# Second phase of an attention and feed-forward kernel: normalising and the output's own-token part move from VectorE to ScalarE, GpSimd's additions are halved, and every engine's step order is new

## The chip, the cores and the metric

The kernel runs on one NeuronCore of a Trainium2 chip (trn2), in one launch. The metric is the device time of one execution in microseconds (us). Five engines run side by side, each through its own list of instructions in order: TensorE (PE; PEld is its weight load), VectorE (DVE), ScalarE (ACT), GpSimd (POOL) and SyncE (SP), which only issues DMAs here. They wait for one another on semaphores.

## The reference

The input is x, 8 batches of 1024 tokens with 256 features. A pre-norm attention (2 query heads, one key and value head of width 128, rotary embedding, causal mask) is added to x; then a feed-forward part on the normalised tokens is added to that. The second is what the change touches:

```python
x = x + _L0_attn_ref(_layernorm(x), ...)
x = x + _L0_ffn_ref(_layernorm(x), ...)

# _L0_ffn_ref(x, ...):
global_context = x.mean(axis=1, keepdims=True)
gf = _global_net(global_context, ...)          # 256 -> 128 -> 64 -> 1, gelu, gelu, sigmoid
out = x
for _ in range(3):
    tf = _coupling_net(out, ...)               # 256 -> 256 -> 128 -> 64 -> 1, gelu x3, sigmoid
    combined = 0.7 * gf + 0.3 * tf
    coupling = 0.1 + adaptive_range * (combined - 0.5) * 2.0
    out = out + coupling * _twist(out)
return out
```

Twisting twice gives minus the vector, so after any cycle `out` is a*x0 + b*twist(x0), where x0 is the normalised token and a and b are two numbers for each token. The output of a token is x + a*x0 + b*twist(x0).

## The kernel before

The first phase (`attention_phase`) is the attention; it ends at about 510 us and is touched only in its last steps. The second phase (`ffn_phase`) takes the 64 tiles of 128 tokens in 16 groups of four tiles (G = 4), group m holding tiles 4m to 4m+3. Two groups are one batch. Each engine walks a list of steps written out by hand, `PERIODS`, once for each n. A step is (kind, ahead, index) and works on group m = n + ahead. Four groups or more are in flight at once, and `x0`, `made`, `rstd` have SLOTS = 4 buffers. The three cycles of one group lie in successive periods. The steps, for one group:

- **stats**: VectorE takes mean and variance of the four tiles (`ffn_moments`, L216 to L222), GpSimd raises the variance to the power -0.5 (`ffn_rstd`, L229).
- **scale**: VectorE writes x0 = (x - mean) * rstd, four instructions of 128x256 (`ffn_scale`, L237). It waits until the slot's former group, m-4, has its output, since that reads the old x0. TensorE's turn waits for all four.
- **turn**: TensorE transposes x0 (L1275), ScalarE copies it out of PSUM as the high half with a row sum (L1076), VectorE subtracts to get the low half (L1157).
- **product** 0 to 3: TensorE multiplies with w1 and its sign-twisted form, six matmuls each (L1291 to L1293); ScalarE copies each result to `made` (L1084).
- **global** 0 to 2: in each second group alone, a chain of three tiny products, each followed by a ScalarE function (L1305, L1310, L1314; L1091, L1094, L1099); VectorE then makes `base_coupling` (L1163).
- **spread** 1, 2: TensorE spreads a and b over the partitions (L1334). It waits for VectorE's `squash` of the cycle before.
- **mix** 1, 2: VectorE multiplies the spread numbers with `made` (L1172, L1175), GpSimd adds the parts over 128x1024 (L1053).
- **gelu1**, **h2**, **h3**: ScalarE's gelu of two halves (L1111), a product (L1345) with a gelu (L1118), a product (L1353, L1357) with a gelu (L1125).
- **dot** and **squash**: GpSimd multiplies with w4 (L1060), VectorE sums (L1183), ScalarE takes a tanh (L1134), VectorE updates a and b in a few instructions of 128x4 (`update_state`, L1225 to L1259).
- **final** 0 to 3, one for each tile: VectorE makes y_part = a*x0 + x (L1196), then adds b*twist(x0) in two instructions of 128x128 (L1204, L1207). After all four, SP stores the group (L1027).

What matters of the order before: VectorE's list is scale(0), stats(1), turn(0), dots, squashes, mix(-1,1), mix(-2,2), final(-3, 0 to 3). TensorE's is turn(0), h3(-2,1), global 0, h3(-3,2), global 1, and in the next period product 0 of the same group, global 2, product 1, both spreads, product 2, h2 of cycle 0, product 3, h3 of cycle 0, h2 of cycles 1 and 2, and the next turn.

## Time and profile before

| | us |
|---|---|
| median of 3 runs (893.6 to 894.84) | 894.32 |
| the profiled execution's own time | 893.9 |
| its span, first to last instruction | 892.4 |
| first phase, to the first instructions of the second | 510.3 |
| turn of the first group to turn of the last (15 periods) | 313.7 |
| from the last turn to the end | 68.4 |

1.5 us of the execution lie outside its span. A row of the trace has a start and a duration in us from the span's start, the engine, the line, the operation, what it writes and reads, and in brackets the idle time ahead of it with what ended that. "PEclk" is the TensorE clock that was granted, as a share of 2.4 GHz: 0.50 is the level of 1.2 GHz. A period here is the time from the start of one turn (L1275) to the next. One where the group of the starting turn closes a batch also has the global steps; it is called a global period below.

### The profile page before, as it was taken

To read this page: it belongs to the slowest core of one execution; us is meant where nothing else is said; L and a number is where in the kernel's file an instruction comes from. 1 tells how busy PE (TensorE), PEld (TensorE's weight loads), DVE (VectorE), ACT (ScalarE), POOL (GpSimd) and SP (SyncE) were. 2 spreads that over 40 slices of the span, in tenths; PEclk is the share of its full clock that TensorE was granted. 3 is DMA by queue.
4 is the path that set the end of the run, shared out by engine and by line. 5 is a ranking of instruction groups with operands and counts; after the bars stand their busy time and mean duration, and the time that the engine had idled before them with its cause. 6 is when DMAs were issued, how large, how long until landed. Compare 5 with 4: busy or idle time off the path is not lost. (4 is left out here: it accounts for less than half of the span.)

```text
span 892.4 us, 13579 instructions
## 1 busy us (share of the span) xinstructions
PE 782.7 (88%) x4240; PEld 638.8 (72%) x4240; DVE 720.0 (81%) x1695; ACT 463.6 (52%) x1020; POOL 365.0 (41%) x375
## 2 busy tenths in 40 slices
PE   4679999999999999999999789888888979898952
PEld 3568888888887888888888666666666757675731
DVE  5879898998998989979988737786977696868675
ACT  2445665556565665565656346554544454445431
POOL 3536634564266345642560014343433333333331
PEclk9899999999999999999999989988988797979775
DMA  6000011001100110011000080000100010101011
GB/s 193 1 1 19 30 49 48 18 31 48 48 25 25 48 48 24 25 48 48 1 1 1 18 265 1 21 27 15 35 24 14 11 48 1 44 5 48 1 48 48
DMA packets 34570, 32.43 MB, mean 36 GB/s; under 512 B 3524, under 2 KB 34244, under 8 KB 34500
## 3 DMA queue, kind: packets, MB, share of 16 engines
q1 hardware_dynamic: 34500, 31.56, 11.1%
q8 instruction: 36, 0.59, 0.3%
q14 instruction: 34, 0.28, 0.1%
HBM read 16.88 MB, written 14.68 MB: 35 GB/s over the span
## 5 line engine op out<-in xcount | busy, mean ns | idle before, releaser
L507 ACT ACTIVATE pT_hi<-bank 128x512 fp32r<-128x512 f32 x192 | 91.2, 492 | 98.7 <-PE bank L846 90.5
L554 ACT ACTIVATE x_all<-scores_ps,neg_max 128x384 f32<-128x384 f32 (+7 forms) x128 | 94.7, 740 | 37.5 <-DVE neg_max L690 37.1
L581 DVE TENSOR_TENSOR pT_lo<-bank,pT_hi 128x512 fp32r<-128x512 f32 x192 | 100.7, 548 | 13.5 <-ACT pT_hi L507 12.4
L846 PE MATMUL bank<-ident,x_all 128*128 128x128 f32 x576 | 91.6, 276 | 20.3 <-DVE pT_lo L581 19.8
L690 DVE CUSTOM_DVE_ANT_0 scores_ps<-scores_ps,x 128x384 f32<-128x384 f32 (+7 forms) x128 | 96.6, 760 | 14.6 <-PE scores_ps L740 14.0
L1345 PE MATMUL cycle_ps<-h,w_sb 128*128 128x512 f32 x192 | 93.5, 624 | 12.5 <-ACT h L1111 12.5
L384 POOL TENSOR_TENSOR rope_a<-x_all,cos_sb 128x384 f32<-128x384 f32 x60 | 61.7, 1028 | 103.2 <-ACT x_all L507 98.9
L846 PEld LDWEIGHTS bank<-ident,x_all 128*128 128x128 f32 x576 | 67.7, 140 | 35.6 <-DVE pT_lo L581 26.3
L1060 POOL TENSOR_TENSOR h_w<-h,w_sb 128x256 f32<-128x256 f32 x48 | 36.5, 762 | 102.6 <-ACT h L1125 102.6
L738 PE MATMUL oT_ps<-pT_hi,v_hi 128*128 128x512 f32 x192 | 75.9, 395 | 1.3 <-issue 1.0
L1345 PEld LDWEIGHTS cycle_ps<-h,w_sb 128*128 128x128 f32 x192 | 36.4, 198 | 47.7 <-issue 25.2
L1053 POOL TENSOR_TENSOR mixed<-part_b,made 128x1024 f32<-128x1024 f32 x16 | 38.1, 2378 | 79.3 <-DVE part_b L1175 79.3
L738 PE MATMUL scores_ps<-k_hi,q_hi 128*128 128x512 f32 (+1 forms) x192 | 69.9, 364 | 0.4 <-ACT x_all L554 0.2
L1291 PE MATMUL made_ps<-x0T_hi,w_hi 128*128 128x512 f32 x128 | 67.2, 525 | 2.8 <-DVE x0T_lo L1157 2.6
L483 POOL TENSOR_TENSOR rope_b<-x_all,sin_sb 128x384 f32<-128x384 f32 x64 | 66.6, 1040 | 1.3 <-ACT x_all L507 0.8
L497 POOL TENSOR_TENSOR rot<-rope_a,rope_b 128x384 f32<-128x384 f32 x64 | 66.2, 1035 | 1.9 <-DVE rope_a L384 1.8
L740 PE MATMUL oT_ps<-pT_hi,v_lo 128*128 128x512 f32 x192 | 66.8, 348 | 0.0
L740 PE MATMUL scores_ps<-k_hi,q_lo 128*128 128x512 f32 (+1 forms) x192 | 66.7, 347 | 0.0
L739 PE MATMUL oT_ps<-pT_lo,v_hi 128*128 128x512 f32 x192 | 66.7, 347 | 0.0
L739 PE MATMUL scores_ps<-k_lo,q_hi 128*128 128x512 f32 (+1 forms) x192 | 66.5, 346 | 0.0
L465 POOL TENSOR_TENSOR rstd<-var_eps,minus_half 128x4 f32<-128x4 f32 x16 | 16.3, 1017 | 117.5 <-DVE var_eps L639 117.5
L1118 ACT ACTIVATE h<-cycle_ps,b_sb 128x512 f32<-128x512 f32 x48 | 33.1, 690 | 59.5 <-PE cycle_ps L1345 59.5
(129 smaller groups left out, 2165.2 us busy)
## 6 DMA issues: line engine op xcount, KB each, us to landing
x_all<-x SPq DMA_DIRECT2D x16, 512.0 KB, 4.0
out<-x_all SPq DMA_DIRECT2D x16, 512.0 KB, 2.9
x<-x_all SPq DMA_DIRECT2D x12, 512.0 KB, 2.9
x_all<-x SPq DMA_DIRECT2D x6, 1024.0 KB, 7.2
x_all<-wqkv SPq DMA_DIRECT2D x1, 512.0 KB, 5.2
sin_sb<-sin_t SPq DMA_DIRECT2D x1, 512.0 KB, 7.0
cos_sb<-cos_t SPq DMA_DIRECT2D x1, 256.0 KB, 5.8
x_all<-wo SPq DMA_DIRECT2D x1, 256.0 KB, 5.4
```

Source lines behind the costliest of these rows:

```text
L483: pool.tensor_tensor(rope_b[:].rearrange("p (c e d) -> p c e d", e=2, d=HALF), qk[:, :, ::-1, :], sin.rearrange("p c (e d) -> p c e d", e= ...
L497: pool.tensor_tensor(rot[:, t, :], rope_a[:], rope_b[:], ALU.add).then_inc(rot_ready, 1)
L507: return nc.scalar.activation(out, in_, ACT.Copy)
L554: nc.scalar.activation(probs[u % 2][:, k, 0:keys], scores_ps[k % 2][:, 0:keys], ACT.Exp, bias=neg_max[:, u * G + k:u * G + k + 1], scale=-1.0,
L581: return dve.tensor_tensor(out, whole, hi.bitcast(F32), ALU.subtract)
L690: dve.tensor_tensor_reduce(out=masked, in0=masked, in1=mask_row[:, T - keys:], scale=-1.0, scalar=LARGEST, op0=ALU.add, op1=ALU.min, accum ...
L738: nc.tensor.matmul(out, stationary[0], moving[0], start=first, stop=False)
L739: nc.tensor.matmul(out, stationary[0], moving[1], start=False, stop=False)
L740: return nc.tensor.matmul(out, stationary[1], moving[0], start=False, stop=last)
L846: mm = nc.tensor.transpose(ps[:, k * P:(k + 1) * P], probs[u % 2][:, k, j * P:(j + 1) * P], ident[:])
L1291: nc.tensor.matmul(ps[:], hi, x0T_hi[:, k, :], start=k == 0, stop=False)
L1345: mm = nc.tensor.matmul(cycle_ps[c][:], f.w2_sb[:, k, :], h1[c][:, k, :], start=k == 0, stop=k == DC - 1)
```

## The change

- `ffn_scale` moves to ScalarE: x0 = rstd*x + shift, as an Identity activation with a scale and a bias for each partition. VectorE makes shift = -mean*rstd first, one instruction of 128x4 for each group (`ffn_shift`). For group 0 both sit at the end of the first phase; ScalarE's four activations stand ahead of its seventh copy of the last unit of scores.
- VectorE's y_part goes. ScalarE writes (1 + a*rstd)*x + a*shift over x, four activations for each group (step **blend**), and VectorE's final adds the twist in place. VectorE makes the scale and the bias in three more instructions of 128x4 at the end of the third squash.
- GpSimd's mix is two additions of 128x512, each with its own semaphore count, and ScalarE's gelu of a half waits for that half.
- All lists have a new order. TensorE's and GpSimd's steps are also counted one or two groups later, which alone moves nothing, since their lists are cyclic. From the turn on, TensorE's is: turn(0), h3(-2,1), h3(-3,2), global 0, 1, 2, product 0, spread of cycle 1, product 1, spread of cycle 2, products 2 and 3, h2 of cycles 0 and 1, h3 of cycle 0, h2 of cycle 2, next turn.

```diff
@@ ffn_scale
-def ffn_scale(dve, f, m, slot, x0, x_tiles):
+def ffn_shift(dve, f, m, slot):
 
     dve.wait_ge(f.rstd_ready, m + 1)
+    dve.scalar_tensor_tensor(out=f.shift[slot][:], in0=f.moments[slot][:, :, 0], scalar=-1.0,
+                             in1=f.rstd[slot][:], op0=ALU.mult,
+                             op1=ALU.mult).then_inc(f.shift_ready, 1)
+
+
+def ffn_scale(act, f, m, slot, x0, x_tiles):
+
+    act.wait_ge(f.shift_ready, m + 1)
     for t in range(G):
-        dve.tensor_scalar(x0[:, t, :], x_tiles[t], f.moments[slot][:, t, 0:1],
-                          f.rstd[slot][:, t:t + 1], ALU.subtract, ALU.mult).then_inc(f.x0_ready, 1)
+        act.activation(x0[:, t, :], x_tiles[t], ACT.Identity, bias=f.shift[slot][:, t:t + 1],
+                       scale=f.rstd[slot][:, t:t + 1]).then_inc(f.x0_ready, 1)
@@ PERIODS
     "tensor": [
-        ("product", -1, 0), ("global", -1, 2), ("product", -1, 1), ("spread", -2, 1),
-        ("spread", -3, 2), ("product", -1, 2), ("h2", -1, 0), ("product", -1, 3), ("h3", -1, 0),
-        ("h2", -2, 1), ("h2", -3, 2), ("turn", 0, 0), ("turn", 0, 1), ("h3", -2, 1),
-        ("global", 0, 0), ("h3", -3, 2), ("global", 0, 1),
+        ("product", -2, 3), ("h2", -2, 0), ("h2", -3, 1), ("h3", -2, 0), ("h2", -4, 2),
+        ("turn", -1, 0), ("turn", -1, 1), ("h3", -3, 1), ("h3", -4, 2), ("global", -1, 0),
+        ("global", -1, 1), ("global", -1, 2), ("product", -1, 0), ("spread", -2, 1),
+        ("product", -1, 1), ("spread", -3, 2), ("product", -1, 2),
     ],
     "scalar": [
-        ("product", -1, 3), ("h3", -1, 0), ("h2", -2, 1), ("h2", -3, 2), ("turn", 0, 0),
-        ("turn", 0, 1), ("global", 0, 0), ("h3", -2, 1), ("h3", -3, 2), ("global", 0, 1),
-        ("squash", -2, 1), ("squash", -1, 0), ("global", 0, 2), ("squash", -3, 2),
-        ("product", 0, 0), ("product", 0, 1), ("gelu1", 0, 0), ("h2", 0, 0), ("gelu1", -1, 1),
-        ("product", 0, 2), ("gelu1", -2, 2),
+        ("gelu1", -3, 2), ("scale", 0), ("h2", -2, 1), ("h3", -1, 0), ("h2", -3, 2), ("turn", 0, 0),
+        ("turn", 0, 1), ("h3", -2, 1), ("product", -1, 3), ("h3", -3, 2), ("global", 0, 0),
+        ("squash", -1, 0), ("global", 0, 1), ("global", 0, 2), ("squash", -2, 1), ("squash", -3, 2),
+        ("product", 0, 0), ("blend", -3), ("product", 0, 1), ("gelu1", 0, 0), ("gelu1", -1, 1),
+        ("product", 0, 2), ("h2", 0, 0),
     ],
     "vector": [
-        ("scale", 0), ("stats", 1), ("turn", 0, 0), ("turn", 0, 1), ("dot", -2, 1), ("dot", -1, 0),
-        ("dot", -3, 2), ("squash", -2, 1), ("global", 0, 2), ("squash", -1, 0), ("squash", -3, 2),
-        ("mix", -1, 1), ("mix", -2, 2), ("final", -3, 0), ("final", -3, 1), ("final", -3, 2),
-        ("final", -3, 3),
+        ("final", -4, 1), ("shift", 0), ("final", -4, 2), ("final", -4, 3), ("stats", 1),
+        ("turn", 0, 0), ("turn", 0, 1), ("dot", -1, 0), ("dot", -2, 1), ("global", 0, 2),
+        ("squash", -1, 0), ("dot", -3, 2), ("squash", -2, 1), ("squash", -3, 2), ("mix", -1, 1),
+        ("mix", -2, 2), ("final", -3, 0),
     ],
     "gpsimd": [
-        ("dot", -1, 0), ("stats", 1), ("dot", -2, 1), ("dot", -3, 2), ("mix", -1, 1),
-        ("mix", -2, 2),
+        ("mix", -3, 1), ("mix", -4, 2), ("dot", -2, 0), ("dot", -3, 1), ("dot", -4, 2),
+        ("stats", 0),
     ],
@@ gpsimd, mix
-                        pool.tensor_tensor(mixed_sb[c][:], part_b[c][:], other,
-                                           ALU.add).then_inc(mix_ready[c], 1)
+                        for k in range(DC):
+                            pool.tensor_tensor(mixed_sb[c][:, k, :], part_b[c][:, k, :],
+                                               other[:, k, :], ALU.add).then_inc(mix_ready[c], 1)
@@ scalar
+                    if kind == "scale":
+
+                        at_least(act, x0_turned, (m - SLOTS + 1) * DC)
+                        at_least(act, y_ready, (m - SLOTS + 1) * (2 * G))
+                        ffn_scale(act, f, m, slot, x0[slot], [x_tile(m, t) for t in range(G)])
+                    if kind == "blend":
+
+                        act.wait_ge(blend_ready, m * 2 + 2)
+                        for t in range(G):
+                            x = x_tile(m, t)
+                            act.activation(x, x, ACT.Identity, bias=blend_shift[:, t:t + 1],
+                                           scale=blend_scale[:, t:t + 1]).then_inc(blended, 1)
@@ scalar, gelu1
                         for k in range(DC):
+                            if c > 0:
+                                act.wait_ge(mix_ready[c], m * DC + k + 1)
@@ vector, final
-                        at_least(dve, y_ready, (m * G + t) * 2)
-                        dve.scalar_tensor_tensor(out=y_part[:], in0=x0[slot][:, t, :],
-                                                 scalar=a_b[:, 0, t:t + 1], in1=x_tile(m, t),
-                                                 op0=ALU.mult, op1=ALU.add).then_inc(y_part_ready, 1)
-                        dve.wait_ge(y_part_ready, m * G + t + 1)
+                        dve.wait_ge(blended, m * G + t + 1)
@@ vector, update_state of the third cycle
+                at_least(dve, blended, m * G)
+                dve.tensor_tensor(x_scale[:], new[:, 0, :], f.rstd[slot][:],
+                                  ALU.mult).then_inc(x_scale_ready, 1)
+                dve.tensor_tensor(blend_shift[:], new[:, 0, :], f.shift[slot][:],
+                                  ALU.mult).then_inc(blend_ready, 1)
                 dve.tensor_scalar(minus_b[:], new[:, 1, :], -1.0, None,
                                   ALU.mult).then_inc(minus_b_ready, 1)
+                dve.wait_ge(x_scale_ready, m + 1)
+                dve.tensor_scalar(blend_scale[:], x_scale[:], 1.0, None,
+                                  ALU.add).then_inc(blend_ready, 1)
```

## Rows read from the trace of the kernel before

**Rows 1.** The page: busy time, share of the span, instructions; the clock in tenths.

```profile
span 892.4 us, 13579 instructions
PE 782.7 (88%) x4240; PEld 638.8 (72%) x4240; DVE 720.0 (81%) x1695; ACT 463.6 (52%) x1020; POOL 365.0 (41%) x375
...
PEclk9899999999999999999999989988988797979775
```

**Rows 2.** Windows, one per period: length, busy us of each engine, PEclk, DMA.

```profile
557.26:579.27 22.01, 19.58 (x96) 14.20 (x94) 16.11 (x36) 11.99 (x27) 7.87 (x6) 0.92 0.03 9
579.27:599.42 20.15, 17.78 (x84) 13.32 (x84) 17.62 (x44) 11.10 (x23) 8.27 (x6) 0.92 0.08 27
599.42:624.38 24.96, 22.63 (x95) 17.35 (x96) 18.01 (x45) 11.35 (x26) 8.22 (x6) 0.79 0.07 22
...
668.13:691.32 23.19, 20.86 (x83) 15.97 (x83) 17.70 (x44) 10.97 (x23) 8.22 (x6) 0.78 0.07 23
...
716.24:735.10 18.86, 16.43 (x84) 11.91 (x84) 17.51 (x44) 10.98 (x23) 8.16 (x6) 1.00 0.09 29
...
sum 266.74, PE 238.32 PEld 179.06 DVE 210.91 ACT 134.75 POOL 98.24; mean PE 19.86 PEld 14.92 DVE 17.58 ACT 11.23 POOL 8.19
```

**Rows 3.** Timeline of the period from 716.24 us.

```profile
716.24 1.10 PE L1275 MATMUL made_ps<-ident,x 128*128 128x128 f32 x8 [2.33 <-DVE x L237]
716.94 0.60 ACT L1076 ACTIVATE x0T_hi<-made_ps 128x512 fp32r<-128x512 f32 x1 [2.30 <-PE made_ps L1275]
...
719.35 0.38 ACT L1125 ACTIVATE h<-cycle_ps 128x256 f32<-128x256 f32 x1 [0.63 <-PE cycle_ps L1357]
...
722.70 0.17 DVE L1259 TENSOR_SCALAR minus_b<-state 128x4 f32<-128x4 f32 x1
...
722.96 1.23 DVE L1175 TENSOR_TENSOR part_b<-cycle_ps,made 128x1024 f32<-128x1024 f32 x1
723.15 1.34 ACT L1111 ACTIVATE h<-made,b_sb 128x512 f32<-128x512 f32 x2
...
726.36 0.56 DVE L1196 SCALAR_TENSOR_TENSOR y_part<-x,state,x_all 128x256 f32<-128x256 f32 x1
726.59 2.58 POOL L1053 TENSOR_TENSOR mixed<-part_b,part_a 128x1024 f32<-128x1024 f32 x1
...
726.95 2.36 DVE L1204 SCALAR_TENSOR_TENSOR x_all<-x,state,y_part 128x128 f32<-128x128 f32 x1
...
730.14 0.35 DVE L1204 SCALAR_TENSOR_TENSOR x_all<-x,state,y_part 128x128 f32<-128x128 f32 x1
730.40 0.35 DVE L1207 SCALAR_TENSOR_TENSOR x_all<-x,minus_b,y_part 128x128 f32<-128x128 f32 x1
...
733.66 1.38 DVE L237 TENSOR_SCALAR x<-x_all,f_moments,f_rstd 128x256 f32<-128x256 f32 x4
...
735.10 1.09 PE L1275 MATMUL made_ps<-ident,x 128*128 128x128 f32 x8 [2.34 <-DVE x L237]
```

**Rows 4.** Windows around the clock's changes, columns as in Rows 2.

```profile
557.26:562.10 4.84, 4.74 (x39) 4.48 (x38) 1.58 (x3) 2.90 (x9) 1.50 (x3) 1.00 0.00 2
562.10:565.50 3.40, 3.40 (x10) 2.35 (x9) 1.96 (x10) 1.41 (x5) 0.61 (x1) 0.50 0.00 0
...
667.92:678.16 10.24, 10.03 (x37) 9.06 (x38) 6.12 (x25) 3.40 (x10) 2.47 (x3) 0.50 0.12 41
```

**Rows 5.** ScalarE by line, 557 to 824 us: count, busy us, mean ns, idle ahead.

```profile
L1111 ACT ACTIVATE h<-mixed,b_sb 128x512 f32<-128x512 f32 x48 | 31.8, 713 | 0.0
L1084 ACT ACTIVATE made<-made_ps 128x512 f32<-128x512 f32 x48 | 28.2, 587 | 10.2 <-PE made_ps L1293 10.2
L1118 ACT ACTIVATE h<-cycle_ps,b_sb 128x512 f32<-128x512 f32 x37 | 25.5, 690 | 41.3 <-PE cycle_ps L1345 41.3
...
L1125 ACT ACTIVATE h<-cycle_ps 128x256 f32<-128x256 f32 x36 | 13.7, 381 | 16.2 <-PE cycle_ps L1357 15.8
```

**Rows 6.** Window from the last turn to the end, columns as in Rows 2.

```profile
824.00:892.38 68.38, 40.93 (x172) 28.65 (x172) 43.68 (x102) 21.00 (x46) 18.17 (x13) 0.71 0.11 36
```

More of the change, by code:

```diff
@@ L204, in __init__ @@
         self.rstd = [sb(f"f_rstd{n}", [P, G]) for n in range(SLOTS)]
+        self.shift = [sb(f"f_shift{n}", [P, G]) for n in range(SLOTS)]
         self.first_x0 = sb("x0_0", [P, G, D])
@@ L563, in do @@
                         r = (FIRST_STEP[u] + j) % PT_RING
+                        if isinstance(b, int) and b == B and j == G + 2:
+                            act.wait_ge(max_ready, B * BATCH_SCORES)
+                            ffn_scale(act, f, 0, 0, f.first_x0,
+                                      [f.x_all[:, t, :] for t in range(G)])
                         act.wait_ge(p_turned, m + 1)
@@ L910, in period_steps @@
             continue
-        if kind in ("stats", "scale") and isinstance(n, int) and n + ahead == 0:
+        if kind in ("stats", "shift", "scale") and isinstance(n, int) and n + ahead == 0:
             continue
@@ L978, in ffn_phase @@
         base_coupling = [sb(f"base_coupling{n}", [P, 1]) for n in range(2)]
-        y_part = sb("y_part", [P, D])
+        x_scale = sb("x_scale", [P, G])
+        blend_scale = sb("blend_scale", [P, G])
+        blend_shift = sb("blend_shift", [P, G])
         made_ps = [psum(f"made_ps{n}", [P, G * P]) for n in range(3)]
@@ L1009, in ffn_phase, with x_tile @@
         minus_b_ready = sem("minus_b_ready")
-        y_part_ready = sem("y_part_ready")
+        x_scale_ready = sem("x_scale_ready")
+        blend_ready = sem("blend_ready")
+        blended = sem("blended")
         y_ready = sem("y_ready")
         y_stored = sem("y_stored")
+        def x_tile(m, t):
+            return x_all[:, m * G + t, :]
         block = ctx.enter_context(nc.Block())
@@ L1148, in do @@
                         ffn_moments(dve, f, m, slot, [x_tile(m, t) for t in range(G)])
-                    if kind == "scale":
-                        at_least(dve, x0_turned, (m - SLOTS + 1) * DC)
-                        at_least(dve, y_ready, (m - SLOTS + 1) * (2 * G))
-                        ffn_scale(dve, f, m, slot, x0[slot], [x_tile(m, t) for t in range(G)])
+                    if kind == "shift":
+                        at_least(dve, f.x0_ready, (m - SLOTS + 1) * G)
+                        ffn_shift(dve, f, m, slot)
                     if kind == "turn":
```

19 lines of the change are left out of this document (7 added, 12 removed).

## The prediction, made before the changed kernel was run

> **What bounds the kernel now.** I read the page first. The span is 892.4 us, and in its last 18 slices, the second phase, TensorE's clock falls to 7 to 9 tenths, while it is full through most of the first [rows 1]. So the second phase has something that the first has not. I then cut it at the turns. From 557.26 to 824.00 us twelve periods take 266.74 us, 22.2 us each, and they are of very different length [rows 2]. The six that are not global take 18.8 us three times, 20.2 us twice and 23.2 us once, 20.0 us in the mean; of the six global ones five take 24.9 to 25.0 us and one takes 22.0 us, 24.45 us in the mean. The clock column sorts them: 1.00, 0.92, 0.78 to 0.80. No engine is full. TensorE is busy 16.43 us of an 18.86 us period at full clock, VectorE 17.5 us, ScalarE 11.2 us, GpSimd 8.2 us.
>
> The timeline says what closes the circle [rows 3]. TensorE does its turn at 716.24 and must stand idle for 2.34 us ahead of the next at 735.10, until VectorE has written x0. VectorE's part: its squashes end at 722.87 (the last small one starts at 722.70 and takes 0.17), the mixes run 722.96 to 726.4, the finals 726.36 to 733.6, the scale 733.66 to 735.04. So the loop is: turn to mix 6.72 us, mixes 3.4, finals 7.2, scale and handing over 1.5: 18.86. The finals take so long because of one instruction: L1204 takes 2.36 us at 726.95 and 0.35 at 730.14. It stands while GpSimd's addition of 2.58 us, from 726.59, runs. Thus VectorE and GpSimd shut each other out.
>
> The same idle time has a second price. The clock is at its lower level (0.50, that is 1.2 GHz) from 667.92 to 678.16, right behind a period's idle time, and once at 562.10 for 3.4 us without idle time: the stretch before is 4.74 us busy of 4.84, but with the turn, the narrow h3 matmuls and the global steps [rows 4]. Half clock costs 4.3 us in a period for 10.24 us of it (23.19 against 18.86), 1.3 for 3.4 us (20.15 against 18.86) [rows 2]: 0.4 us for each us of it.
>
> **The change, part by part, over one period at full clock.**
>
> *Scale.* VectorE loses 1.38 us. But x0 has four buffers, and scale(m) still waits for all four finals of m-4: the link stays in the loop. ScalarE's price isn't in the trace. Nearest rows: 381 ns for 128x256 without a pointer operand; a bias pointer adds 690 - 587 = 103 ns at 128x512; the whole 128x512 from SBUF is 713 [rows 5]. So 381 + 2 x 103 = 587 ns, less some 90 of overlap (two L1111 of 0.713 take 1.34 us together [rows 3, 5]), is 0.50 us each. Bounds are 0.38 and 0.71. Four are 2.1 us (1.5 to 2.9), in place of 1.38.
>
> The Trainium skill (ScalarE: Activation LUTs, Rules for kernel authors) says to do add and multiply on VectorE, not on ScalarE. By that rule this move loses time, and the rows agree that an instruction gets dearer. What counts here is in whose list it stands; and ScalarE has 11 us of work in 22.
>
> *y_part and blend.* VectorE loses 4 x 0.48 to 0.56, 2.1 us with the handing over, out of the loop [rows 3]. ScalarE gains 4 x 0.50 = 2.0 us ahead of product 1's copy. ScalarE's load becomes 11.2 + 4.1 = 15.3 us. blend waits for the third squash, so product 1's copy and the gelu of cycle 0 come some 3 us later than their data, and TensorE, which wants that gelu after four products, waits about 0.8 us there; that is inside the slack TensorE has. The four added small ones on VectorE at 0.17 us each, three in the chain of the third squash, add 0.4 us to it, and shift adds 0.2 to the finals.
>
> *Halves of mix.* Two of about 1.25 us instead of one of 2.4 to 2.6. Fixed cost of the second: 0.1 to 0.2 us, hidden. The gelu of the first half may start 1.2 us earlier; that isn't on the loop, the finals are. The shut-out of VectorE stays, since finals and addition meet as before, and they exclude each other for the same total of 2.5 us. Bounds: nothing gained, or 1.2 us gained if a half falls elsewhere. I take nothing.
>
> The Trainium skill (SBUF — State Buffer, Who interferes with whom) states that a VectorE instruction with two SBUF inputs and a GpSimd one that reads SBUF exclude each other for the whole instruction. L1204's 2.36 us agrees. By that rule the new finals are still open to it.
>
> *Order.* ScalarE now does three evacuations (h2, h3, h2: 0.65 + 0.35 + 0.65) between scale and turn, and product 3's between two h3. Before, its turn copy began 0.70 us behind the turn; now it begins 1.65 us behind the scale, and the h3 of cycle 2 is done 0.65 us later than at +3.49 [rows 3]. For that TensorE waits 0.6 us ahead of product 0.
>
> The loop now: turn to mix 6.72 + 0.65 + 0.4 = 7.8; mixes 3.5; finals 7.15 - 2.1 - 0.25 (a small shut-out with dot, which has moved away) + 0.2 = 5.0; scale 2.1 and handing over 0.1. That is **18.5 us** against 18.86. The bounds of ScalarE's price make it 17.9 to 19.2. TensorE needs 16.5, so it waits 2.0 us a period still, but in three pieces under 0.9 us, and only 0.4 ahead of the turn.
>
> *Global periods.* TensorE's global 0, 1, 2 now stand in a row, with nothing between them to cover the trips to ScalarE and back, and ScalarE's copy of product 3, a h3 and a tanh stand in between. I count base_coupling, and with it the mix, 1.4 us later: 19.9 us at full clock. The six global periods before are 20.6 by the same reckoning (22.0 - 1.4).
>
> *The clock.* With only 0.4 us idle ahead of the turn I expect no fall in the other periods: 18.5. In the global ones turn, narrow matmuls and waits are some 6 us of light work, and the fall at 562.10 came so: I expect it in each, four times for 3.4 us (21.3) and twice for 10.24 (24.2). Twelve periods: 6 x 18.5 + 4 x 21.3 + 2 x 24.2 = 244.6, that is **-22 us**.
>
> *Ends.* At the end of the first phase four activations on ScalarE hold back two copies of scores, which VectorE's 1.38 us didn't: +0.5. Between 510 and 557 the first scale waits behind an h2: +0.6 by estimate, against as much gained by four products in a row: 0 in all. SP's list is the old one, and no DMA is moved. Behind the last turn, 68.4 us [rows 6]: one global period, -1.5 as above; three joins of mix and gelu in the drain, 0.6 each (second half 1.25 + one gelu 0.7 in place of two gelus); last finals without y_part, -1.4, small ones +0.4. Say -4.
>
> Sum: 893.9 - 22 - 4 = 868 for the profiled kind of execution; the median lies 0.4 above the profiled one's own time. I forecast **868 us**.
>
> **Rivals.**
> 1. *The clock stays full.* If global periods don't fall either: 6 x 18.5 + 6 x 19.9 = 230.4, -36, ends -5: **853**. For it: idle pieces under 1 us. Against: 562.10.
> 2. *The clock falls as often as now.* 6 others: 18.5 + (2 x 1.4 + 4.3)/6 = 19.7; global: 19.9 + (5 x 4.3 + 1.4)/6 = 23.7; sum 260, -6.5, ends -3: **884**. For it: a turn, two h3 and two waits are still light work.
> 3. *Slower: TensorE's idle time only moves behind the turn and keeps the clock low.* The wait for product 0, with h3 and turn ahead of it, makes each period long: 22.8 and 24.2 give 282, +15, ends -2: **907**. It decides from a mean period of 22.5 us. For it: ScalarE's list now stands between turn and product 0. Against: idle time falls from 2.34 to 2.0 us and is split.
> 4. *Nothing.* A dearer scale (0.71 each, +0.75 us a period) with rival 2 takes the gain: about 893.
>
> **Numbers.** Forecast 0.45, its own range 857 to 877; rival 1 0.18; rival 2 0.20; rival 3 0.13; rival 4 0.04. A measurement of this kernel tells 0.2% (1.8 us) from no change. Faster 0.83, same 0.04, slower 0.13. For 8 in 10 I go from 846 (rival 1 with the cheap activation) to 888.
>
> **What would show it.** Right: L237 gone, TensorE's idle time ahead of L1275 under 1 us and ended by ScalarE; periods without global steps near 18.5 at PEclk 1.00; new activations of about 0.5 to 0.6 us; a final's instruction still stretched to about 1.3 us beside a half addition; ScalarE busy about 15 us a period. Wrong: half clock in the periods without global steps; finals ending with GpSimd out of the way (then under 17.9); new waits on ScalarE for blend or scale that end with VectorE and are longer than 1 us; another table load.

## The result: 841.8 us against 894.6, and the profile after

The changed kernel takes 841.83 us (median of 4 runs, 840.5 to 842.96), the kernel before 894.58 us beside it (893.6 to 895.0). The ratio is 0.9411, with an interval from 0.9391 to 0.9431. The forecast was 868 us with a range from 846 to 888, so the time fell by twice what was forecast, 53 us instead of 26, and came out 4 us below the range. The forecast had the sign and the mechanism, but it had the length of the loop wrong, and what the clock does in the global periods.

The page of the changed kernel, to be read beside [rows 1]: busy times, and the clock by slice.

```profile
span 839.0 us, 13716 instructions
PE 752.3 (90%) x4240; PEld 612.5 (73%) x4240; DVE 658.6 (78%) x1631; ACT 525.6 (63%) x1148; POOL 365.7 (44%) x407
...
PEclk9899999999999999999999998999999999999975
```

Between the first phase and the drain the clock row now hardly leaves 9. TensorE does the same 4240 matmuls in 752 us instead of 783, because fewer of them run at half clock. VectorE has lost 61 us and ScalarE has gained 62.

The windows by period of the changed kernel (columns as in [rows 2]); of twelve, six are shown, and the first, third and fifth of these are global.

```profile
558.59:578.45 19.86, 19.16 (x96) 14.39 (x94) 14.08 (x40) 15.10 (x35) 8.33 (x8) 0.91 0.07 23
578.45:595.31 16.86, 16.46 (x85) 11.91 (x84) 14.03 (x39) 14.81 (x32) 8.32 (x8) 1.00 0.11 37
...
667.21:687.08 19.87, 19.17 (x96) 14.38 (x94) 13.99 (x40) 15.19 (x35) 8.29 (x8) 0.91 0.07 23
687.08:703.94 16.86, 16.45 (x84) 11.92 (x84) 14.02 (x39) 14.88 (x32) 8.34 (x8) 1.00 0.11 37
703.94:722.38 18.44, 17.74 (x96) 13.23 (x95) 13.99 (x40) 15.26 (x35) 8.35 (x8) 1.00 0.08 28
722.38:739.12 16.74, 16.42 (x84) 11.86 (x83) 14.04 (x39) 14.69 (x32) 8.32 (x8) 1.00 0.10 34
...
sum 217.50, PE 210.85 PEld 155.36 DVE 166.59 ACT 179.89 POOL 99.85; mean PE 17.57 PEld 12.95 DVE 13.88 ACT 14.99 POOL 8.32
```

Twelve periods take 217.50 us instead of 266.74. The six without global steps take 16.7 to 17.1 us, all at PEclk 1.00. Of the six global ones two take 18.44 us at full clock and four 19.87 at 0.91. In a period of 16.86 us TensorE is busy 16.45: the engine that waited for VectorE before is now the bound itself.

The timeline of the period from 687.08 us shows the circle of [rows 3] again, and that it no longer closes on TensorE.

```profile
686.93 0.67 ACT L1154 ACTIVATE h<-cycle_ps,b_sb 128x512 f32<-128x512 f32 x1
...
687.08 1.09 PE L1308 MATMUL made_ps<-ident,x 128*128 128x128 f32 x8
687.50 0.36 ACT L1161 ACTIVATE h<-cycle_ps 128x256 f32<-128x256 f32 x1
687.77 0.67 ACT L1154 ACTIVATE h<-cycle_ps,b_sb 128x512 f32<-128x512 f32 x1
...
688.34 0.58 ACT L1112 ACTIVATE x0T_hi<-made_ps 128x512 fp32r<-128x512 f32 x1
...
689.15 1.00 PE L1390 MATMUL cycle_ps<-w_sb,h 128*128 128x64 f32 x8
...
690.22 0.41 ACT L1161 ACTIVATE h<-cycle_ps 128x256 f32<-128x256 f32 x1
...
690.49 0.47 PE L1324 MATMUL made_ps<-x0T_hi,w_hi 128*128 128x512 f32 x1 [0.35 <-ACT made L1120]
...
693.08 0.16 DVE L1281 TENSOR_TENSOR state<-state,scaled 128x4 f32<-128x4 f32 x1
...
693.56 1.22 DVE L1210 TENSOR_TENSOR part_b<-cycle_ps,made 128x1024 f32<-128x1024 f32 x1
...
693.69 2.08 ACT L1105 ACTIVATE x_all<-x_all,blend_shift,blend_scale 128x256 f32<-128x256 f32 x4 [0.80 <-DVE blend_scale L1292]
...
697.13 0.43 DVE L1234 SCALAR_TENSOR_TENSOR x_all<-x,state,x_all 128x128 f32<-128x128 f32 x1
...
697.37 2.60 POOL L1077 TENSOR_TENSOR mixed<-part_b,part_a 128x512 f32<-128x512 f32 x2
697.49 1.36 DVE L1237 SCALAR_TENSOR_TENSOR x_all<-x,minus_b,x_all 128x128 f32<-128x128 f32 x1
...
698.77 1.35 DVE L1234 SCALAR_TENSOR_TENSOR x_all<-x,state,x_all 128x128 f32<-128x128 f32 x1
...
700.38 0.34 DVE L1234 SCALAR_TENSOR_TENSOR x_all<-x,state,x_all 128x128 f32<-128x128 f32 x1
...
700.91 0.34 DVE L1234 SCALAR_TENSOR_TENSOR x_all<-x,state,x_all 128x128 f32<-128x128 f32 x1
701.17 0.34 DVE L1237 SCALAR_TENSOR_TENSOR x_all<-x,minus_b,x_all 128x128 f32<-128x128 f32 x1
...
701.59 2.07 ACT L247 ACTIVATE x<-x_all,f_shift,f_rstd 128x256 f32<-128x256 f32 x4
702.17 1.94 PE L1378 MATMUL cycle_ps<-h,w_sb 128*128 128x512 f32 x4
...
703.94 0.82 PE L1308 MATMUL made_ps<-ident,x 128*128 128x128 f32 x6
```

The turn at 703.94 has no bracket: its matmuls wait for nothing. Its x0 was ready at 703.66, 0.28 us earlier, and TensorE was still at L1378. (Only the weight load ahead of it, which has no row here, was held for x0, until 703.72.) The one wait of TensorE left in the period is 0.35 us at 690.49, for ScalarE. Read as in the prediction, the loop is: turn to mix 6.48 us, mixes 3.57, finals 4.38 (697.13 to 701.51), scale and handing over 2.15. That is 16.6 us, just under the 16.8 us of TensorE's own circle, its 16.45 us of work and the wait of 0.35.

### The profile page after: what moved, and what is told of

It reads as the page before. It is cut to its first block and busy times, and to the rows that moved or that the text cites. A ratio compares the mean times of both kernels' runs of the same rounds, so it can differ in the third digit from the quotient of the medians.

```text
span 839.0 us, 13716 instructions
## 1 busy us (share of the span) xinstructions
PE 752.3 (90%) x4240; PEld 612.5 (73%) x4240; DVE 658.6 (78%) x1631; ACT 525.6 (63%) x1148; POOL 365.7 (44%) x407
## 5 line engine op out<-in xcount | busy, mean ns | idle before, releaser
L1378 PE MATMUL cycle_ps<-h,w_sb 128*128 128x512 f32 x192 | 94.2, 628 | 11.3 <-ACT h L1147 11.1
L1378 PEld LDWEIGHTS cycle_ps<-h,w_sb 128*128 128x128 f32 x192 | 35.9, 198 | 49.4 <-issue 30.2
L1324 PE MATMUL made_ps<-x0T_hi,w_hi 128*128 128x512 f32 x128 | 57.9, 452 | 4.6 <-ACT made L1120 3.0
L1192 DVE TENSOR_TENSOR x0T_lo<-made_ps,x0T_hi 128x512 fp32r<-128x512 f32 x32 | 20.6, 686 | 52.4 <-ACT x0T_hi L1112 52.4
L517 ACT ACTIVATE x_all<-bank 128x512 f32<-128x512 f32 x64 | 38.1, 596 | 34.1 <-PE bank L754 34.1
```

The lines of the kernel that those rows point to most:

```text
L517: return nc.scalar.activation(out, in_, ACT.Copy)
L1378: mm = nc.tensor.matmul(cycle_ps[c][:], f.w2_sb[:, k, :], h1[c][:, k, :], start=k == 0, stop=k == DC - 1)
```

## The experiments

Sixteen runs were made, one of them the changed kernel once more, each with the kernel before on the same chip. The chips differ by up to 0.5%, so times of different groups are best compared by their ratios. The kernel before took 889.83 us beside the order alone, the old order, the filled kernel and the whole additions, 893.52 beside the rest of part 2, 892.62 beside two and six extra instructions, TensorE's old list and the drain, 893.39 beside the last four. "Period" means one without global steps, where nothing else is said.

**1. Where the 53 us come from.** First the parts: all operations as before in the new order, all new operations in the old order, and the kernel before with nothing but extra matmuls on the idle TensorE.

*Order alone* (scale back on VectorE, y_part back, whole additions):

```diff
@@ scalar, against the changed kernel's list
-        ("gelu1", -3, 2), ("scale", 0), ("h2", -2, 1), ("h3", -1, 0), ("h2", -3, 2), ("turn", 0, 0),
+        ("gelu1", -3, 2), ("h2", -2, 1), ("h3", -1, 0), ("h2", -3, 2), ("turn", 0, 0),
...
-        ("product", 0, 0), ("blend", -3), ("product", 0, 1), ("gelu1", 0, 0), ("gelu1", -1, 1),
+        ("product", 0, 0), ("product", 0, 1), ("gelu1", 0, 0), ("gelu1", -1, 1),
@@ vector
-        ("final", -4, 1), ("shift", 0), ("final", -4, 2), ("final", -4, 3), ("stats", 1),
+        ("final", -4, 1), ("final", -4, 2), ("final", -4, 3), ("scale", 0), ("stats", 1),
```

> The instructions of before (scale and y_part on VectorE, whole additions), in the new order; VectorE's scale stands behind the last final. Theory A (the period is the longer of TensorE's work, 16.5 us, and the loop turn - squashes - mix - finals - scale - turn; the clock falls only behind idle time of TensorE or in global steps): loop 6.3 + 3.65 + 4.4 + 2.1 for y_part + 1.5 for scale = 17.95, so 1.1 us idle ahead of the turn, a clock that falls in global periods alone: 850 to 860 us. Rival B (the order does nothing, the moved instructions do it all): 888 to 895. Rival C (the order does it all): 842 to 845.

It took 886.38 us against 889.83 before, ratio 0.994 (0.9901 to 0.9978). That is outside all three ranges, between theory A and rival B. A period at full clock:

```profile
668.78:687.20 18.42, 16.41 (x84) 11.87 (x84) 17.54 (x44) 11.19 (x23) 8.12 (x6) 1.00 0.09 30
```

Theory A had 17.95 us for it with 1.1 us idle ahead of the turn. It is 18.42 with 1.91 idle, and the clock falls in four of the six periods, where A had it fall in global ones alone.

*New operations in the old order* (scale ahead of the turn and blend ahead of product 1 in ScalarE's list, shift in scale's old place on VectorE; GpSimd's power stands behind the dots, since its wait for the blend's scale asks for that; all else in the lists as before):

```diff
@@ scalar
-        ("gelu1", -3, 2), ("scale", 0), ("h2", -2, 1), ("h3", -1, 0), ("h2", -3, 2), ("turn", 0, 0),
+        ("product", -1, 3), ("h3", -1, 0), ("h2", -2, 1), ("h2", -3, 2), ("scale", 0),
...
-        ("product", 0, 0), ("blend", -3), ("product", 0, 1), ("gelu1", 0, 0), ("gelu1", -1, 1),
+        ("product", 0, 0), ("blend", -3), ("product", 0, 1), ("gelu1", 0, 0), ("h2", 0, 0), ("gelu1", -1, 1),
```

> The instructions of after (scale and blend on ScalarE, halves) in the order of before; blend stands behind product 0, scale right ahead of ScalarE's turn copy, GpSimd's power behind the dots, which blend forces. Theory A: loop 6.7 + 0.4 (small instructions) + 3.6 + 4.6 + 2.2 = 17.5, idle 1 us ahead of the turn: 848 to 858 us. Rival B (the moved instructions do it all): 842 to 845. Rival C (the order does it all): 885 to 895.

It took 933.85 us, ratio 1.0496 (1.0445 to 1.0546): slower than either kernel, and far outside all three ranges. Its timeline, at a full-clock period of 21.3 us:

```profile
754.90 2.08 ACT L1105 ACTIVATE x_all<-x_all,blend_shift,blend_scale 128x256 f32<-128x256 f32 x4 [1.02 <-DVE blend_scale L1292]
...
758.88 1.98 PE L1378 MATMUL cycle_ps<-h,w_sb 128*128 128x512 f32 x4 [2.12 <-ACT h L1147]
...
762.27 0.34 DVE L1237 SCALAR_TENSOR_TENSOR x_all<-x,minus_b,x_all 128x128 f32<-128x128 f32 x1
...
767.33 2.06 ACT L247 ACTIVATE x<-x_all,f_shift,f_rstd 128x256 f32<-128x256 f32 x4
...
769.44 0.33 PE L1308 MATMUL made_ps<-ident,x 128*128 128x128 f32 x1 [2.74 <-ACT x L247]
```

The blend stands ahead of cycle 0's gelu, and TensorE waits 2.12 us for that. VectorE's finals end at 762.6, but scale starts at 767.33, since it is queued behind gelus whose matmuls come late. So neither half of the change, as run here, is worth much alone (-3 us and +44 us); together they give -53. The +44 holds for this one way of putting the new steps into the old lists: the blend alone in the old order, with scale left on VectorE, was not run, so how much a better place for them would save there is open.

*The kernel before with its idle time filled*: ten matmuls of 128x384 whose result nobody reads, ahead of the turn's wait.

```diff
+                        if c == 0 and isinstance(n, int) and 4 <= n < NGROUPS:
+                            for _ in range(10):
+                                nc.tensor.matmul(global_ps[:, P:4 * P], f.w1_hi[0][:, 0, 0:P],
+                                                 f.w1_hi[0][:].rearrange("p c n -> p (c n)")[:, 0:3 * P],
+                                                 start=True, stop=True)
                         pe.wait_ge(f.x0_ready, m * G + G)
```

> The kernel before, with ten matmuls of 128x384 on weights, their product used by nobody, ahead of TensorE's wait for x0 in each turn from group 4 on: about 1.7 us at full clock inside 2.3 us of idle time. Nothing else is changed. Theory A (the idle time has a second price, the clock): the clock stays full in periods without global steps, 18.9 us each, global ones 20.6 to 22: 862 to 875 us, faster with more work. Rival (the clock falls for another reason, the light matmuls of turn and h3): as before or slower, 894 to 910.

It took 863.36 us against 889.83, ratio 0.9703 (0.9655 to 0.975), as theory A has it. Two of its windows, columns as in [rows 2]:

```profile
658.35:677.18 18.83, 18.14 (x93) 13.67 (x93) 17.50 (x44) 10.98 (x23) 8.17 (x6) 1.00 0.09 29
677.18:697.62 20.44, 19.84 (x106) 15.04 (x106) 17.93 (x45) 11.42 (x26) 8.23 (x6) 1.00 0.08 27
```

The loop is as long as before (18.83 us), but every period without global steps is now at full clock, with TensorE idle 0.60 us ahead of the turn instead of 2.34. So about 26 of the 53 us are the price of the clock alone. The rest is the loop: from 18.86 to 16.85 us and from 20.4 to 18.4 us is 2.0 us in each of twelve periods, 24 us, less 1.4 for one short fall of the clock more in the changed kernel's global periods (four against three); the ends give what is left.

**2. Which of the operations matters.** From the changed kernel one was undone at a time.

*Scale back on VectorE* (behind the last final; all else as changed):

```diff
@@ vector
-        ("final", -4, 1), ("shift", 0), ("final", -4, 2), ("final", -4, 3), ("stats", 1),
+        ("final", -4, 1), ("shift", 0), ("final", -4, 2), ("final", -4, 3), ("scale", 0), ("stats", 1),
```

> The changed kernel with scale on VectorE again (four instructions behind the last final); blend, halves and order stay. Theory A (period = the longer of TensorE's work and the loop): in the changed kernel VectorE's finals end 14.4 us behind the turn, and TensorE wants x0 at 16.8; 1.4 us of scale on VectorE fit, and ScalarE's copies come earlier: 836 to 842 us, idle ahead of the turn under 0.3 us. Rival (taking scale off VectorE was needed): 850 or more.

839.85 us (839.65 to 840.3), as theory A has it, where the changed kernel, run beside it, took 842.75 (841.98 to 844.12). *The changed kernel again:*

> The changed kernel once more, as the yardstick for the three beside it on one chip: 840 to 844 us.

The ratios to before are 0.9402 (0.9367 to 0.9437) and 0.9437 (0.9406 to 0.9468). Moving scale was not needed; the version without that move is the fastest measured, by 0.3%, though the intervals of the ratios overlap. Its period:

```profile
686.83:703.56 16.73, 16.40 (x84) 11.85 (x83) 16.30 (x47) 12.81 (x27) 8.35 (x8) 1.00 0.11 37
```

The Trainium skill (ScalarE: Activation LUTs, Rules for kernel authors) gives adds and multiplies to VectorE. The rows agree for this step: four such instructions take 2.07 us on ScalarE (L247) and took 1.38 us on VectorE [rows 3]. The next experiment shows where the rule didn't decide.

*y_part back on VectorE* (no blend, scale stays on ScalarE):

```diff
-                        dve.wait_ge(blended, m * G + t + 1)
+                        dve.scalar_tensor_tensor(out=y_part[:], in0=x0[slot][:, t, :],
+                                                 scalar=a_b[:, 0, t:t + 1], in1=x_tile(m, t),
+                                                 op0=ALU.mult, op1=ALU.add).then_inc(y_part_ready, 1)
+                        dve.wait_ge(y_part_ready, m * G + t + 1)
...
```

> The changed kernel with y_part on VectorE again (no blend); scale on ScalarE, halves and order stay. Theory A: the finals get 2.1 us longer, the loop 16.6 + 2.1 - 0.3 = 18.4 us; TensorE idle 1.6 us ahead of the turn, clock falls in global periods and some others: 862 to 880. Rival (ScalarE, relieved of 2 us, gives it back): 842 to 850.

898.62 us, ratio 1.0067 (1.0034 to 1.0101), outside the expected range. TensorE is idle 2.1 us ahead of each turn again, and no period is at full clock (20.3 to 21.5 us, PEclk 0.84 to 0.92). The blend is what takes the loop below TensorE's work: added last, it is worth 56 us (898.62 to 842.75), more than the whole change. The two kernels with scale on VectorE say the same: 0.994 of the time before with y_part on VectorE (order alone, with whole additions), 0.940 with the blend.

*Whole additions on GpSimd* (one of 128x1024 instead of two halves):

```diff
-                        for k in range(DC):
-                            pool.tensor_tensor(mixed_sb[c][:, k, :], part_b[c][:, k, :],
-                                               other[:, k, :], ALU.add).then_inc(mix_ready[c], 1)
+                        pool.tensor_tensor(mixed_sb[c][:], part_b[c][:], other[:],
+                                           ALU.add).then_inc(mix_ready[c], DC)
```

> The changed kernel with each addition of GpSimd whole again, 128x1024. Theory A: the gelus of mixed halves have slack, and finals and addition exclude each other for the same total: 842, within 2 us. Rival (the halves let gelu and finals in earlier, and that counts): 846 or more.

844.22 us, ratio 0.9492 (0.9437 to 0.9546); its periods without global steps are 16.8 to 17.1 us, the same, and they could hardly show more, since TensorE bounds them. The time lies just outside theory A's 842 within 2. Behind the last turn it takes 64.7 us instead of 62.95, but so do others with the halves (64.8 in the next experiment). The intervals of the ratios overlap (0.9406 to 0.9468 for the changed kernel again), so these runs don't tell the halves' worth from nothing. In its periods one final alone is stretched beside GpSimd's addition:

```profile
697.85 2.47 DVE L1236 SCALAR_TENSOR_TENSOR x_all<-x,minus_b,x_all 128x128 f32<-128x128 f32 x1
```

*Global steps apart* (global 0 between the two h3, 1 and 2 behind the second, on both engines):

```diff
@@ tensor; ScalarE's list alike
-        ("turn", -1, 0), ("turn", -1, 1), ("h3", -3, 1), ("h3", -4, 2), ("global", -1, 0),
+        ("turn", -1, 0), ("turn", -1, 1), ("h3", -3, 1), ("global", -1, 0), ("h3", -4, 2),
```

> The changed kernel with global 0 between the two h3 and global 1 behind them, in TensorE's and ScalarE's lists. Theory A: TensorE loses two waits of 0.35 us in global periods and the light stretch gets shorter, so the clock falls less often (four of six before): 835 to 841. Rival (the wait is only moved to product 0, and the clock falls on the light matmuls whatever their order): 841 to 844.

845.29 us, ratio 0.946 (0.9418 to 0.9501), above both ranges: global periods of 18.7 us at full clock instead of 18.44, and the clock falls in four of six as it did. Putting them in a row costs nothing.

**3. The length of the loop.** Extra VectorE instructions of 128x256, output unused, ahead of the last final make the changed kernel's loop longer and leave all else alone.

```diff
...
+                        if t == 3:
+                            at_least(dve, spare_ready, m * 6)
+                            for s in range(6):
+                                dve.tensor_scalar(spare[:, s, :], f.w1_hi[0][:, 0, :].bitcast(F32), 1.0,
+                                                  None, ALU.mult).then_inc(spare_ready, 1)
```

Two, and then six:

> The changed kernel with 2 extra VectorE instructions (128x256, about 0.33 us each) ahead of the last final of each group; their output is not used. They lengthen the loop turn, mix, finals, scale by 0.66 us, to about 17.2 us at full clock. Theory A (a period is the longer of TensorE's own work, 16.8 us, and the loop; the clock stays full while little idle time stands ahead of the turn): about 0.4 us a period more, 16 periods, 846 to 851 us, periods without global steps 17.2 to 17.3 us at full clock. Rival (loop and TensorE's work are not separate bounds, every us added counts from the first): 842 + 16 x 0.66 = 853 us. Rival C (any idle time brings clock falls): above 860 us.

> The same with 6 extra instructions, 2.0 us, which makes the loop about 18.6 us, the length that the prediction forecast for it. Theory A: TensorE stands idle 1.7 to 2.0 us ahead of each turn; by the order-only run that is enough to bring clock falls in most periods, so periods of 18.6 us at full clock and 20 to 23 us with falls, 870 to 900 us in all. Rival (the clock would have stayed full at the forecast's length in the periods without global steps, as the prediction's sum has it): 18.5 to 18.6 in all six of those, 862 to 870 us.

They took 848.29 us (ratio 0.9498, 0.947 to 0.9527) and 857.24 us (0.960, 0.9575 to 0.9625). The first is as theory A has it; the second missed both ranges, because the extra instructions are cheaper than assumed. The row of six, and the windows of a period with two and with six:

```profile
673.64 1.29 DVE L1231 TENSOR_SCALAR spare<-w_hi 128x256 f32<-128x256 f32 x6
```

```profile
693.32:710.36 17.04, 16.63 (x84) 11.78 (x84) 14.41 (x41) 14.67 (x32) 8.33 (x8) 1.00 0.10 32
```

```profile
659.83:677.66 17.83, 16.63 (x83) 11.77 (x83) 15.20 (x45) 14.61 (x32) 8.31 (x8) 1.00 0.09 31
```

One costs 1.29 / 6 = 0.215 us. 17.04 - 2 x 0.215 = 16.61 and 17.83 - 6 x 0.215 = 16.54: the loop of the changed kernel is 16.6 us, by the timeline and by these two.

Now the lengths that the prediction had given the loop, and that of the kernel before:

> The changed kernel with 9 extra VectorE instructions (128x256, output unused) ahead of the last final. In the runs with 2 and 6 of them each took 0.215 us of the loop, and the period at full clock was 17.04 and 17.84 us, so that the loop without any is 16.6 us. With 9 it is 16.6 + 1.9 = 18.5 us, the length that the prediction gave it, and TensorE stands idle 1.7 us ahead of the turn. Theory A (the prediction's sum at its own loop length): no clock fall in the periods without global steps, 18.5 us each, global ones with short falls, 866 to 876 us in all. Theory B (1.7 us idle is enough to bring falls, as the 1.9 us of the order-only run were): falls in most periods, 20 to 23 us each, 885 to 905 us.

> The same with 12 extra instructions: loop 16.6 + 2.6 = 19.2 us, idle 2.3 us ahead of the turn, as the kernel before has it. Theory B: falls in most periods, often long ones, a mean period of 22 to 23.5 us, 900 to 920 us. Rival (the kernel before loses its clock through something else than this idle time): periods of 19.2 and 21 us with short falls alone, 875 to 885 us.

Nine made it 866.34 us (0.9717, 0.966 to 0.9774) and twelve 895.43 (1.002, 0.9997 to 1.0042). Windows of nine, and of twelve:

```profile
661.62:680.08 18.46, 16.62 (x83) 11.78 (x83) 15.71 (x48) 14.61 (x32) 8.34 (x8) 1.00 0.09 30
```

```profile
583.58:604.22 20.64, 18.26 (x84) 13.41 (x84) 16.77 (x51) 14.73 (x32) 8.32 (x8) 0.92 0.08 27
671.12:692.76 21.64, 19.36 (x83) 14.54 (x84) 16.67 (x51) 14.68 (x32) 8.33 (x8) 0.84 0.08 26
```

| extra instructions | idle ahead of the turn, us | period, us | periods with half clock, of the 6 | time, us |
|---|---|---|---|---|
| 0 | 0 | 16.85 | 0 | 841.8 |
| 2 | 0.25 | 17.04 | 0 | 848.3 |
| 6 | 1.05 | 17.83 | 0 | 857.2 |
| 9 | 1.66 | 18.46 | 1 | 866.3 |
| 12 | 2.27 | 19.1 to 21.6 | 4 | 895.4 |

With a loop of 18.46 us the kernel takes 866 us, about what the prediction forecast for 18.5, and inside the range of theory A. Its four executions lie between 863 and 873 us, the profiled one at 869. Twelve came out between its two theories, with falls in most periods but few long ones. From nine to twelve the loop grows by 0.65 us, 8 us over twelve periods, and the time by 29: there the idle time begins to cost the clock as well. The order-only kernel of part 1 has the same full-clock period as nine, 18.42 us, with the idle time in one piece of 1.91 us, where nine has 1.66 and 0.36; its clock falls in four of six periods and it takes 886 us. Whether the 0.25 us or the one piece makes that difference was not separated.

**4. Which list the new operations need.** One engine's list at a time was put back to the old order in the changed kernel: TensorE's, ScalarE's (as in the old-order kernel of part 1), VectorE's.

```diff
@@ tensor
-        ("product", -2, 3), ("h2", -2, 0), ("h2", -3, 1), ("h3", -2, 0), ("h2", -4, 2),
...
+        ("spread", -3, 2), ("product", -1, 2), ("h2", -1, 0), ("product", -1, 3), ("h3", -1, 0),
+        ("h2", -2, 1), ("h2", -3, 2), ("turn", 0, 0), ("turn", 0, 1), ("h3", -2, 1),
...
@@ vector, in the third kernel
...
-        ("turn", 0, 0), ("turn", 0, 1), ("dot", -1, 0), ("dot", -2, 1), ("global", 0, 2),
-        ("squash", -1, 0), ("dot", -3, 2), ("squash", -2, 1), ("squash", -3, 2), ("mix", -1, 1),
...
+        ("shift", 0), ("stats", 1), ("turn", 0, 0), ("turn", 0, 1), ("dot", -2, 1), ("dot", -1, 0),
+        ("dot", -3, 2), ("squash", -2, 1), ("global", 0, 2), ("squash", -1, 0), ("squash", -3, 2),
...
```

> The changed kernel with TensorE's list alone in the order of before (spreads and h2 between the products, global steps apart), the lists of ScalarE and VectorE as changed. Theory A (the gain of the order lies in the three lists fitting together): TensorE's first h2 stands behind three products and waits for a gelu that ScalarE now makes later, so idle time comes back: 845 to 870 us. Rival (the gain lies in the lists of ScalarE and VectorE alone): 842 us as the changed kernel.

> The changed kernel with ScalarE's list alone in the order of before, scale ahead of the turn and blend ahead of product 1 as in the kernel with all lists old. Theory A (ScalarE's list is where the old order fails the changed operations: the blend ahead of the gelu of cycle 0, and scale behind product 3 and three evacuations): 880 to 930 us, TensorE idle over 1.5 us ahead of its turn, ended by ScalarE's scale. Rival (TensorE's list is what costs in the old order): under 860 us.

> The changed kernel with VectorE's list alone in the order of before (first squash behind the second, dots ahead of each other as before, all four finals of a group in a row ahead of shift and stats). Theory A (VectorE's list costs little, since both orders put the same operations between turn and mix): mix starts 0.2 to 0.4 us later behind the turn and the loop is 16.8 to 17.1 us: 842 to 850 us. Rival (the squash of cycle 0 behind the second dot holds the spread and so the mix back by over 1 us): 860 us or more.

They took 879.92 us (0.9855, 0.9824 to 0.9885), 953.5 (1.0681, 1.0638 to 1.0724) and 855.78 (0.9582, 0.9547 to 0.9617). In the first two theory A has the place right, but both cost more than its ranges; the third is between its two theories. The waits of TensorE that the three bring back, one row of each timeline:

```profile
676.99 1.98 PE L1378 MATMUL cycle_ps<-h,w_sb 128*128 128x512 f32 x4 [1.69 <-ACT h L1147]
```

```profile
705.06 1.09 PE L1308 MATMUL made_ps<-ident,x 128*128 128x128 f32 x8 [2.74 <-ACT x L247]
```

```profile
663.86 0.65 PE L1367 MATMUL cycle_ps<-ident,state 128*128 128x128 f32 x4 [0.92 <-DVE state L1250]
```

With TensorE's old list the first h2 stands behind three products instead of four, and waits 1.69 us for a gelu that the blend has delayed. With ScalarE's old list scale is queued behind everything, as in part 1, and TensorE also waits 2.0 us for a gelu ahead of an h2. With VectorE's old list the squash of cycle 0 comes behind the second. The mix starts 0.42 us later behind the turn (6.90 against 6.48), about as theory A has it, but that isn't what makes the period 17.7 us: the spread waits 0.92 us for that squash, the rival's mechanism. ScalarE's list is the one that costs most, 112 us.

**5. The drain.** Behind the last turn the changed kernel still takes 62.95 us, much of it at half clock. From there on eight unused matmuls were put ahead of each spread and h2, in the kernel with scale on VectorE, where that stretch takes 62.92 us at 0.74 without them.

```diff
+                        if n >= NGROUPS + 1:
+                            for _ in range(8):
+                                nc.tensor.matmul(global_ps[:, P:4 * P], f.w1_hi[0][:, 0, 0:P],
+                                                 f.w1_hi[0][:].rearrange("p c n -> p (c n)")[:, 0:3 * P],
+                                                 start=True, stop=True)
                         pe.wait_ge(h1_ready[c], m * DC + DC)
...
```

> The changed kernel with scale on VectorE and, from the drain on only, 8 extra matmuls (128x384, result unused) ahead of each spread and each h2 wait, so that TensorE isn't idle there. Theory A (the drain, 62.9 us behind the last turn with some 30 us of it at half clock, is partly bound by the clock): 4 to 8 us less than the 840 us of that kernel, 832 to 836 us, and the periods before the drain unchanged. Rival (the drain is bound by the chain of gelus, mix and finals and not by TensorE's clock): 839 to 843 us.

844.0 us (840.2 to 846.1), ratio 0.9447 (0.9413 to 0.9481), against 839.85 and 0.9402 (0.9367 to 0.9437) without them, on another chip. Theory A's gain of 4 to 8 us didn't come, and the median is 1 us above the rival's range. The window behind the last turn, of the changed kernel and of this one:

```profile
776.09:839.04 62.95, 37.25 (x173) 25.29 (x171) 35.74 (x98) 31.32 (x66) 19.28 (x19) 0.74 0.10 34
```

```profile
776.10:842.14 66.04, 47.10 (x245) 36.66 (x243) 35.78 (x98) 30.99 (x64) 18.61 (x18) 0.88 0.10 33
```

The clock is higher, 0.88 against 0.74, and the drain isn't shorter but 3 us longer. Of these 3 us, 2 may have nothing to do with them: with the same lists and no extra matmuls it takes 62.9 us in some profiles and 64.8 to 65.0 in others (global steps apart; two and six extra instructions). That it is bound by a chain over VectorE, GpSimd and ScalarE, in which TensorE's clock matters little, fits this and was not tested further.

## Why the prediction missed, step by step

- **The loop before, and its second price: right.** The idle time ahead of the turn cost the clock; filling it alone gave 26 us.
- **Turn to mix, 7.8 us: wrong, and the largest error in the loop.** It measured 6.48, 1.3 less. The prediction added 0.65 us for ScalarE's evacuations and 0.4 for the new small instructions to the old 6.72. The turn's copy did begin late, 1.26 us behind the turn instead of 0.70. Behind the scale it is 1.41 us (686.93 to 688.34), where 1.65 was forecast: the three evacuations in a row start 0.57, 0.27 and 0.57 us apart, less than their own durations. But the last h3 was done at +3.55 us, hardly later than the old +3.49. The reason stood in [rows 3]: ScalarE had waited 0.63 us for TensorE ahead of that very h3, and a wait absorbs what comes ahead of it. The matmuls that it waits for end at +3.07 in both kernels (689.15 and 718.31, each with 1.00). The small instructions cost next to nothing: from the start of the squash's last instruction to the mix it is 0.48 us (693.08 to 693.56) where it was 0.45 (722.51 to 722.96). And from the end of the last h3 to that instruction it is 2.45 us instead of 2.78; the squash of cycle 0 now stands ahead of the last dot, and with VectorE's old list (part 4) it is 2.87. The two rows of the kernel before:

```profile
718.31 1.00 PE L1357 MATMUL cycle_ps<-w_sb,h 128*128 128x64 f32 x8
...
722.51 0.16 DVE L1256 TENSOR_TENSOR state<-state,scaled 128x4 f32<-128x4 f32 x1
```

- **Finals, 5.0 us: 0.6 too long.** They measured 4.38. From one tile's final to the next it is 0.53 us (700.38 to 700.91) where it was 1.17 (730.14 to 731.31), so a tile's y_part took 0.64 us of the list, and all four 2.5 us and not 2.1. The new shift takes 0.07 us of the list and not 0.2, and a stretched final, 0.47 us over its plain 0.35, had been taken at 0.25; against these goes 0.1 us that the two stretches beside the halves cost more than the one before. These are rows of the kernel before:

```profile
731.31 0.35 DVE L1204 SCALAR_TENSOR_TENSOR x_all<-x,state,y_part 128x128 f32<-128x128 f32 x1
731.58 0.82 DVE L1207 SCALAR_TENSOR_TENSOR x_all<-x,minus_b,y_part 128x128 f32<-128x128 f32 x1
```

- **Scale 2.1, mixes 3.5: right** (2.07 for four, 590 ns each by themselves; 3.57). That scale was worth moving was wrong, as part 2 shows. The loop of 18.5 us was thus 16.6.
- **TensorE's work: in the prediction, but not as a bound.** It had "TensorE needs 16.5" and never asked what happens if the loop comes out shorter. The period is 16.85, TensorE's 16.45 busy, a wait of 0.35 for ScalarE and little else. This is also why a further gain on VectorE or ScalarE, as in the version of 839.85 us, gives next to nothing.
- **Halves and shut-out: right.** Nothing in the periods. L1237 and L1234 take 1.36 and 1.35 us beside the two halves, where L1204 took 2.36 beside one whole [rows 3]: 2.0 us over the plain 0.35 in both; with whole additions in the changed kernel one final takes 2.47, 2.1 us over it (part 2). The Trainium skill (SBUF — State Buffer, Who interferes with whom) says that such a pair excludes each other for a whole instruction; the rows agree, and splitting one side of it only splits the wait.
- **Global periods, 19.9 us at full clock: 18.44.** That is the same error of the loop.
- **The clock: half right.** No fall in the periods without global steps, as forecast. In the global ones four short falls, as forecast, but none of the two long ones. With the loop's error this is the whole miss over twelve periods: six others 9.9 us (18.5 against 16.85), four global ones 5.7 (21.3 against 19.87), two global ones 11.5 (24.2 against 18.44), 27.1 in all. Some 18.6 of these are the loop's and 8.6 the two long falls, 4.3 each, that never came. And the reason given for the full clock, 0.4 us idle ahead of the turn and 2.0 us a period in three pieces, was not what happened: nothing is idle ahead of the turn, and 0.35 us in the period.
- **Ends, -4 us: right in sum** (510.33 to 509.50, 46.93 to 49.09, 68.38 to 62.95: -4.1), and by luck: the first phase was forecast 0.5 longer and is 0.8 shorter, the three periods before the twelve were to stay and are 2.2 longer in all, the drain was forecast about 4.3 shorter and is 5.4.
- **The rivals.** The first (the clock stays full) came nearest with 853 us. The third (slower, through idle time behind the turn) did not come: behind the turn the changed kernel waits only 0.35 us. Two of the kernels with old lists are slower than before, but through idle time ahead of the turn or ahead of an h2.

With nine extra instructions the changed kernel has the prediction's loop, and takes 866 us. So from the loop's length on, the sum stood nearly; the step from the lists to that length failed. In part that too is luck: its twelve periods take 240.6 us where the sum had 244.6, with one fall in a plain period that the sum didn't have and without the two long ones that it had, and its 1.66 us of idle time ahead of the turn are not the prediction's 0.4.

## What to carry to other kernels

When a change puts work ahead of an instruction that waits, subtract the wait that the trace shows in brackets before adding the work; and when a loop through other engines gets shorter, compare it with the busy time of the engine it returns to, which is the next bound. Price idle time of TensorE twice, and measure the second price by filling the gap with unused matmuls in the old kernel: that takes a few lines and told here that half the gain was clock. Try operations and the order that they need together: here the new order alone gave next to nothing, and the new operations in the old order, in the one placing that was run, a loss.

## What the hardware showed unexpectedly

- Idle time and clock are not in proportion. With 0.25, 1.05 and 1.66 us idle ahead of each turn, five or all six of the periods without global steps stayed at full clock; at 2.27 us four of six lost it, and 0.65 us more loop cost 29 us of time.
- The clock also falls without a long wait of TensorE ahead of it. In the changed kernel it is at its lower level from 673.6 to 677.0 us, 6.4 us after the start of a turn that had waited for nothing. In these 6.4 us TensorE is busy 5.69, with a turn, two narrow h3 and the global steps, and its two waits are of 0.35 us. Four of six such periods show it and two, with the same instructions, don't.

```profile
667.21:673.60 6.39, 5.69 (x44) 5.29 (x43) 2.86 (x8) 4.58 (x15) 2.17 (x3) 1.00 0.01 3
673.60:677.00 3.40, 3.40 (x12) 2.71 (x11) 2.71 (x14) 2.50 (x6) 1.45 (x2) 0.50 0.00 0
```

- A higher clock isn't always worth having: with unused matmuls in the drain the clock rose from 0.74 to 0.88 and gained nothing (66.0 us, against 62.9 to 65.0 without them).
